# The last block's k and v computed in absent steps of the recurrent block's first and last turns

## What is computed

```python
x = _L0_xattn_ref(x, ctx_2048, ...)    # grouped attention, layer norm
x = _L1_xattn_ref(x, ctx_2048, ...)    # non-local block with batch statistics
x = _L2_xattn_ref(x, ctx_2048, ...)    # recurrent block: projections, scan, feed-forward
x = _L3_xattn_ref(x, ctx_2048, ...)    # cross attention and MLP

def _L3_xattn_ref(hidden_states, encoder_hidden_states, ...):
    q = (layer_norm(hidden_states, ln1_w, ln1_b) @ q_w + q_b)     # 16 heads of 32
    k = (encoder_hidden_states @ k_w + k_b)                       # the context, not x
    v = (encoder_hidden_states @ v_w + v_b)
    attn = softmax(where(mask, q k^T / sqrt(32), finfo.min))
    hidden = (attn @ v) @ cproj_w + cproj_b + hidden_states
    y = gelu(layer_norm(hidden, ln2_w, ln2_b) @ fc_w + fc_b) @ proj_w + proj_b
    return hidden + y
```

## Time and profile before

| what | us |
|---|---|
| median of 3 runs | 4407.73 |
| range of the 3 runs | 4401.81 to 4412.48 |
| the profiled execution | 4404.54 |
| its span | 4402.8 |
| PE busy in it | 4084.0 (93%) |
| DVE busy | 2325.2 (53%) |
| ACT busy | 1502.5 (34%) |
| POOL busy | 1423.2 (32%) |

### The profile page before, as it was taken

The page is one execution under the profiler, slowest core; times in us unless marked ns, Lnnn a source line. Parts: engine busy times, 40 slices in busy tenths (PEclk is TensorE's granted clock), DMA queues, the critical chain, the costliest instruction groups (busy, mean ns, idle before and its releaser), DMA issues. The chain is left out here.

```text
span 4402.8 us, 79945 instructions
## 1 busy us (share of the span) xinstructions
PE 4084.0 (93%) x30944; PEld 2520.5 (57%) x30944; DVE 2325.2 (53%) x2689; ACT 1502.5 (34%) x2622; POOL 1423.2 (32%) x1181
## 2 busy tenths in 40 slices
PE   6999999994799999999999997789999999999998
PEld 5666666663566666666666664345444444544443
DVE  4666666662577767776666774343333333333320
ACT  2555555552333443344333332112222221222210
POOL 2433333431554555455444542121111111111110
PEclk8999999997899999999999998899999999999999
DMA  3121212113001000010000000300000000000000
GB/s 100 59 68 66 68 58 68 61 44 124 21 19 38 26 26 26 26 36 26 26 26 26 26 25 11 147 21 1 30 20 10 30 1 30 1 30 8 22 10 10
DMA packets 102765, 161.50 MB, mean 37 GB/s; under 512 B 17264, under 2 KB 34800, under 8 KB 101936
## 3 DMA queue, kind: packets, MB, share of 16 engines
q1 hardware_dynamic: 102448, 156.59, 10.5%
HBM read 106.20 MB, written 41.94 MB: 34 GB/s over the span
## 5 line engine op out<-in xcount | busy, mean ns | idle before, releaser
L1410 DVE COPY_PREDICATED b_A<-b_mask,b_pS 128x2048 f32<-128x2048 uint32 x128 | 458.3, 3580 | 184.2 <-PE b_pS L1124 183.2
L1862 PE MATMUL c_pR<-c_proj_w,c_fcT 128*128 128x512 f32 x1024 | 459.5, 597 | 7.5 <-ACTq L1701 3.8
L1796 PE MATMUL c_pR<-c_xT,c_fc_w 128*128 128x512 f32 x1024 | 458.2, 595 | 7.5 <-PEq L1701 2.4
L695 POOL TENSOR_TENSOR a_S<-a_S,a_negmax 128x2048 f32<-128x2048 f32 x64 | 231.1, 3610 | 500.0 <-DVE a_negmax L629 500.0
L2013 POOL TENSOR_TENSOR c_S<-c_S,c_negmax 128x1024 f32<-128x1024 f32 x64 | 121.4, 1897 | 701.3 <-DVE c_negmax L1960 701.3
L1563 POOL TENSOR_TENSOR b_R<-b_R,b_Wh 128x512 f32<-128x512 f32 x192 | 228.4, 1190 | 356.9 <-PE b_pS L1124 356.5
L1986 DVE TENSOR_TENSOR c_res<-c_res,c_pR 128x512 f32<-128x512 f32 x128 | 88.0, 687 | 482.8 <-PE c_pR L1862 449.4
L1124 PE MATMUL b_pS<-b_R,b_kT 32*128 32x128 f32 x7168 | 271.2, 288 | 77.1 <-ACT b_A L1264 36.3
L1796 PEld LDWEIGHTS c_pR<-c_xT,c_fc_w 128*128 128x128 f32 x1024 | 191.4, 190 | 244.5 <-issue 240.7
L1873 ACT ACTIVATE c_fcT<-c_pR,c_vec 128x512 f32<-128x512 f32 x128 | 88.0, 687 | 698.3 <-PE c_pR L1796 658.1
L1862 PEld LDWEIGHTS c_pR<-c_proj_w,c_fcT 128*128 128x128 f32 x1024 | 189.7, 190 | 238.4 <-issue 228.0
(11 more groups left out here) (228 smaller groups left out, 7921.5 us busy)
## 6 DMA issues: line engine op xcount, KB each, us to landing
a_c<-ctx SPq DMA_DIRECT2D x16, 512.0 KB, 4.0
a_x<-x SPq DMA_DIRECT2D x16, 512.0 KB, 5.0
a_kexp<-a_kT SPq DMA_DIRECT2D x512, 16.0 KB, 1.8
a_xl<-x SPq DMA_DIRECT2D x32, 256.0 KB, 2.6
a_cl<-ctx SPq DMA_DIRECT2D x32, 256.0 KB, 2.8
mid_x<-a_xl SPq DMA_DIRECT2D x32, 256.0 KB, 2.9
mid_wy<-a_wy SPq DMA_DIRECT2D x32, 256.0 KB, 2.1
b_x1g<-mid_x SPq DMA_DIRECT2D x16, 512.0 KB, 4.1
```

What stands on the lines that cost most here:

```text
L695: nc.gpsimd.tensor_tensor(S[n % 2][:, :, :], S[n % 2][:, :, :], negmax[n % 2][:, :].unsqueeze(2).to_broadcast([P, RH, T]), ALU.add)\
L1410: nc.vector.copy_predicated(A[:, :, :].rearrange("p q (n two h) -> p q n two h", two=2, h=h)[:, :, :, 1, :], masks[h][:, :].bitcast(U32).r ...
L1796: mm = nc.tensor.matmul(bank, w[:, c, at * P:at * P + P], src[:, c, :], start=(c == 0), stop=(c == KC - 1))
L1862: mm = nc.tensor.matmul(bank, fcT[part % 2][:, m, g * T:g * T + T], proj_w[:, KC * part + m, :], start=(m == 0), stop=(m == KC - 1))
```

## The change

`phase_a` stores every transposed context tile `cT` in DRAM. `phase_b` computes all 32 K and 32 V fills of the last layer in places of absent steps: 24 in turns -1, 0 and 1 (groups 0 to 2), 40 in turns 15 and 16 (groups 3 to 7). Such a unit takes an absent step's bank of the ring; PE fills it from the stored `cT` rows, the step's own engine drains it with the bias, and SP stores it. V units take places that DVE drains, K units places that ACT drains. For the early units k_w and v_w lie in the buffers of `Wfk` and `Wfr`, the context rows in those of `Wfv` and `Wo`, and the weights `Wo`, `Wfk`, `Wfr`, `Wfv` are loaded after the last early unit (turn 1). For the late units k_w and v_w are loaded over `Wk` and `Wr` after turn 14's scan. `phase_c` loads finished k and v instead of the context, and loses the steps `cT`, `k` and `v`.

The units by place: in turn -1, seven before the step n1 (two V, then five K), V after shift, V before a0, two K before k0, one V each inside k0 and after td, two K before b1, three K at fk0, fk1 and fr0; in turn 0 four V (fv0, fv1, o0, o1); in turn 1 two V (fv0, fv1). In turn 15, 21 units in slots 3 to 15 (none in slots 0 to 2, 4, 8, 16 and 17). In turn 16, eleven before the step gate, one K each at k0 and td, two K at w and two V at b0 before n2, two V at b1 after n2.

```diff
+            def store_cT(j):
+                wait(out(j, "cT", 1))
+                sp.dma_start(dram["cT"][bass.ds(j.times(1), 1), :, :, :].rearrange("b p k n -> p (b k) n"), cT[:, :, :]).then_inc(*cT_stored.up(16))
...
                 if has(i + 1):
                     load_mask(i + 1, 1 - par)
                     spread_k(i + 1, 1 - par)
+                    store_cT(i + 1)
...
+                        if s == "cT":
+                            act.wait_ge(*cT_stored(j + -1, 16))
...
+    EARLY, LATE = (-1, 0, 1), (N - 1, N)
+    OUT_SLOTS = 6
+    def absent(turn):
+        return [(name, who) for kind, step in table if not 0 <= turn + LAG[kind] < N for name, who in fills(kind, step)]
+    def share(turns, first, groups):
+        left = {g: {"K": list(range(KC)), "V": list(range(GC))} for g in range(first, first + groups)}
+        order = []
+        for turn in turns:
+            for name, who in absent(turn):
+                window = sorted(left)[:2]
+                for kind in "VK" if who == "dve" else "K":
...
+            def load_kv(side):
+                sp.dma_start(kv_k[side][:, :, :], dram["L3_xattn_k_w"].rearrange("(k p) n -> p k n", p=P)).then_inc(*kv_weights["K"].up(16))
+                first = sides[side][0][3][1]
+                load_group(side, first)
+                sp.dma_start(kv_v[side][:, :, :], dram["L3_xattn_v_w"].rearrange("(k p) n -> p k n", p=P)).then_inc(*kv_weights["V"].up(16))
+                sp.dma_start(kv_rows[side], dram["rows_c"][:, 0:D]).then_inc(*kv_weights["V"].up(16))
+                load_group(side, first + 1)
...
             load(Turn(None))
+            load_kv(0)
             load_state(Turn(None), 0)
...
+            turn(Turn(None, add=N - 2), 0, True)
+            before = Turn(None, add=N - 1)
+            wait(x2_saved.all(before))
...
+            wait(S_.full(before + -1, "s", G - 1, SLOTS - 1))
+            load_kv(1)
...
+            def unit(at, name, side, n):
+                _, _, _, (kind, group, m) = sides[side][n]
+                for free in Ring.ready(R_, at, name):
+                    pe.wait_ge(*free)
+                bank = pR[:, R_.at[name] % RING, :]
+                pe.wait_ge(kv_weights[kind].sem, (16 if kind == "K" else 32) * (side + 1))
+                pe.wait_ge(*groups_loaded(side, group))
+                if kind == "K":
+                    for h in range(2):
+                        for c in range(KC):
+                            mm = nc.tensor.matmul(bank[:, h * TOK:h * TOK + TOK], kv_k[side][:, c, m * P:m * P + P], half_of(side, group, h)[:, c, :],
+                                                  start=(c == 0), stop=(c == KC - 1))
+                else:
+                    h, at_ = divmod(m * T, TOK)
+                    for c in range(KC):
+                        mm = nc.tensor.matmul(bank, half_of(side, group, h)[:, c, at_:at_ + T], kv_v[side][:, c, :], start=(c == 0), stop=(c == KC - 1))
+                mm.then_inc(*R_.filled.up())
...
-    TABLE = """F0 hb F1 cT w1 F2 k0 F3 k1 n1 R0 k2 q0 R1 k3 s0 q1 R2 v0 s1 R3 v1 F4 t0 s2 v2 F5 v3 t1 p0 s3 F6 F7 t2 p1
+    TABLE = """F0 hb w1 F1 F2 F3 n1 R0 q0 R1 q1 s0 R2 s1 R3 F4 t0 s2 F5 t1 p0 s3 F6 F7 t2 p1
...
+            def load_k(j):
+                if (j + -1).exists():
+                    wait(scored(j + -1, NU))
+                sp.dma_start(kT[:, :, :], dram["k"][bass.ds(j.times(1), 1), :, :, :].rearrange("b p k n -> p (b k) n")).then_inc(*k_loaded.up(16))
...
                 if has(i + 2):
-                    wait(full(i + 1, "n2", KC - 1))
-                    load_context(i + 2)
+                    load_k(i + 2)
+                    load_v(i + 2)
                     wait(limit_sign(i + 1, 1))
                     load_mask(i + 2)
```

More of the change, by code:

```diff
@@ L876, in take_groups, with unit_out, stores_done, run @@
             return [pR[:, R_.bank(name, g), :] for g in range(G)]
-        def run(eng, scan, project, finish, who=""):
+        def unit_out(eng, at, name, side, n):
+            eng.wait_ge(*R_.filled(at, R_.at[name] + 1))
+            nth, slot = divmod(n, OUT_SLOTS)
+            if nth:
+                eng.wait_ge(*stores(slot, side, nth))
+            return pR[:, R_.at[name] % RING, :], kv_slots[side][n % OUT_SLOTS]
+        def stores_done(eng):
+            for slot in range(OUT_SLOTS):
+                eng.wait_ge(*stores(slot, 1, 0))
+        def run(eng, scan, project, finish, who="", unit=None):
             def skip(at, kind, step):
@@ L900, in turn @@
                         else:
+                            if unit is not None and static and i.add == 1 and (kind, step) == ("f", "gn_mean"):
+                                stores_done(eng)
                             (project if kind in "pl" else finish)(i + LAG[kind], (par + LAG[kind]) % 2, step)
@@ L986, in turn, with mixed, has @@
                         load_state(i + 2, par)
-            for i in (-1, 0, 1):
-                turn(Turn(None, add=i), i % 2, True)
+            def mixed(n):
+                i = Turn(None, add=n)
+                def has(j):
+                    return 0 <= j.add < N
+                for kind, step in table:
+                    if not has(i + LAG[kind]):
+                        for name, _ in fills(kind, step):
+                            if (n, name) in unit_at:
+                                store_unit(n, name)
+                            if (n, name) == sides[0][-1][0:2]:
+                                wait(R_.filled(i + 1, R_.at[name] + 1))
+                                for w in ("Wo", "Wfk", "Wfr", "Wfv"):
+                                    load_weights(loaded_f, W[w], "L2_%sT" % w)
+                    if (kind, step) == ("p", "stats"):
+                        if has(i + -2):
+                            store(i + -2)
+                        if has(i + -1):
+                            back(i + -1)
+                        if has(i + 1):
+                            save(i + 1)
+                    if (kind, step) == ("p", "w") and has(i + 2):
+                        load(i + 2)
+                        if has(i):
+                            load_state(i + 2, n % 2)
+            for n in EARLY:
+                mixed(n)
             with sp.Fori(0, (N - 4) // 2) as reg:
@@ L992, in _ @@
                     turn(Turn(reg, 2, 2 + u), u, False)
-            for i in range(N - 2, N + 2):
-                turn(Turn(None, add=i), i % 2, True)
+            turn(Turn(None, add=N - 2), 0, True)
+            before = Turn(None, add=N - 1)
+            wait(x2_saved.all(before))
+            wait(xn_ready[0].all(before))
+            wait(R_.full(before, "w", 1))
+            wait(R_.full(before, "r", 1))
+            wait(r_joined.all(before + -1))
+            wait(S_.full(before + -1, "s", G - 1, SLOTS - 1))
+            load_kv(1)
+            for n in LATE:
+                mixed(n)
+            turn(Turn(None, add=N + 1), 1, True)
+            for slot in kv_stored:
+                sp.wait_ge(slot.sem, slot.seen)
             sp.wait_ge(*stored.all(Turn(None, add=N - 1)))
@@ L1304, in finish, with unit @@
                     nc.scalar.activation(rt[:, g, :], bank, ACT.Tanh, scale=0.5).then_inc(*R_.emptied["act"].up())
-            run(act, scan, project, finish, "act")
+            def unit(at, name, side, n):
+                _, _, _, (kind, group, m) = sides[side][n]
+                if side and n < OUT_SLOTS:
+                    act.wait_ge(*xm_ready.all(Turn(None, add=N - 1)))
+                bank, dst = unit_out(act, at, name, side, n)
+                nc.scalar.activation(dst, bank, ACT.Identity, bias=col("L3_xattn_k_b", m)).then_inc(*R_.emptied["act"].up())
+            run(act, scan, project, finish, "act", unit)
         @block.vector
@@ L1813, in step @@
                     linear(j, s, W["q_w"], n, xT1, "n1")
[L1814 to L1818 removed]
                 elif s[0] == "s":
                     c, pair_ = divmod(n, 2)
+                    if n == 0:
+                        pe.wait_ge(*k_loaded(j, 16))
                     pe.wait_ge(*(masked(j, n) if n else masked.before(j)))
```

169 lines of the change are left out of this document (114 added, 55 removed).

## The result

The changed kernel takes 4332.16 us (median of 4 runs, 4323.25 to 4340.87) against 4404.77 for the kernel before beside it: a ratio of 0.9834, 95% interval 0.9816 to 0.9852. The forecast was 4328. The profiled execution took 4340.87 us (span 4339.1) and is the longest of the four, so its parts add up to more than the median.

What follows compares the result with a forecast made beforehand. PE's stream bounds phase_c's turn 0 and phase_b's middle turns; a DVE, ACT and POOL chain bounds phase_b's edges. 4404.54 - 220.6 (phase_c) + 141.3 (phase_b) = 4325.2 us profiled, median 3.2 above: 4328 (4302 to 4366).

Steps and rivals of the forecast that it cites:

- Turn -1: phase_b's turn -1 grows by 44.2 us (38 to 55), with n1 coming 26.2 us later.
- turns 0 and 1: phase_b's turns 0 and 1, with six units, grow by 1 us each (0 to +8 and -1 to +7).
- A unit: PE's time for one moved K or V unit: 3.5 us, so 224 us for 64 (219 to 238).
- Turns 15 and 16: phase_b's end: turn 15 grows by 47.5 us (43 to 57), turn 16 by 47.6 (44 to 56).
- The cT stores: phase_a's 16 stores of cT cost nothing; if SP were late, under 0.5 us a turn, 8 in all.
- phase_c's middle turns: Seven turns of phase_c lose 204.3 us of fills, less 2 us for newly exposed waits: 202.3 us gained.
- phase_c's first stage: phase_c's turn -1, up to the fourth score step: a gain of 18.3 us (14 to 22).
- rival A: PE's clock falls to 0.66 in phase_c's first stage: +28 us, 4356; chance 0.07.
- B: phase_c's middle turns are no longer PE's; n1 or transposes wait 5 us a turn: +35, 4363; chance 0.08.
- C: phase_b's edges hide nothing and the moved units cost all 224 us: 4411, no change; chance 0.03.
- D: In phase_c, loads of k and v delay the x rows by 20 us beyond slack each turn: 4468; chance 0.03.
- E: phase_b's edges hide more: all 99.4 us idle and some 12 of clock go, growth 112, 4299; chance 0.04.

Runs made afterwards that it cites:

- quarter units: The changed kernel with each of the 64 units doing only the first of its four input blocks, all loads, drains and stores kept: 4199.78 us.

## Why the prediction was right, by its own steps

**What bounds the kernel.** Right: the moved work hid where PE had idled, and only there. Turn -1 grew 2.1 us more than the sum, turns 0 and 1 3.8 less. Part of how near the total came is luck, though: the changed kernel's own executions lie 18 us apart, and between executions the end of the same phase_a moves by up to 9 us.

**A unit.** A V unit of 8 records takes 3.6 us in the clean stretches (two in 7.03), as did a K unit: 3.5 was right.

**Turn -1.** The first unit came at 67.35 of 67 (behind phase_a's end moved by 3.5), n1 at +26.4 of +26.2. Behind n1 it was +19.9 of +18.0: I had POOL's 3.2 us stay (2.38 measured). Of idle time 11.8 us went and not 12.7, and by difference the clock gave back 6.8 and not 7.8.

**Turns 15 and 16.** +45.6 and +49.8 of +47.5 and +47.6: their sum is off by 0.3. The quarter units show how it comes about: the first quarter of the late work, 35 us, cost 4.3, since it fell into idle time, and the rest 91.7 of 105, since little was left to fill. I had expected 87 for that rest, from the same working.

**The cT stores** at nothing: right within 7 us, which is what that run can tell.

**phase_c's middle turns.** The fills went with their price and n1 stayed clear as worked out (2.8 us for "some 3"). The term that was mis-sized is "2 us for newly exposed waits": it was 10.2 (204.3 less 194.1). The six waits before F0 are 6.9 of it, the slow clock of turn 0's first four F fills 1.9 (15.94 us for 14.0, and 14.0 when the same kernel ran again). The waits come from k and v in flight as the loop closes. No row of before shows them: there the q8 packets came as well, nine a turn, and those of the loop's end had landed 0.5 us or more before F0.

**phase_c's first stage.** 12.1 for 18.3, the largest miss for its size (that of the middle turns is 8.2 of 202.3). I let POOL start 3.6 us earlier for 1.4 MB less ahead of cproj_w; it started 1.4 earlier, counted from the last fv (35.2 for 36.6), which is 2.2 of the 6.2 us missed. From there to q0 it was 7.7 us for 6.8, and from q0 to the fourth score step 21.6 for 18.4. The clock accounts for these two: rival A happened in small. The clock in 10 us before n1 and the 10 behind it, in the changed kernel and then in the kernel before:

```profile
2951.50:2961.50 10.00, 0.00 (x0) 0.00 (x0) 2.20 (x5) 0.00 (x0) 2.40 (x4) 0.50 1.04 417
2961.50:2971.50 10.00, 9.00 (x24) 5.51 (x24) 4.95 (x2) 3.11 (x4) 4.63 (x1) 0.55 1.02 397
```

```profile
2807.10:2817.10 10.00, 7.72 (x20) 2.98 (x17) 7.17 (x19) 1.38 (x2) 2.49 (x4) 1.00 1.04 411
2817.10:2827.10 10.00, 9.59 (x34) 5.00 (x35) 4.96 (x2) 4.00 (x6) 4.64 (x1) 1.00 1.02 404
```

Without cT and k there PE idles 31 us before n1, and what follows runs at a granted clock of 0.50 to 0.55, the lower level (1.2 GHz) for most of it. The removed fills had also borne the start themselves (cT took 3.24 us at 2804.20, while POOL still waited). The price here is the 3.68 less 1.97 and the 5.81 less 3.6, about 4 us, and not the 28 of rival A, since the clock was back by the second q fill (3.67 us). It fell once more behind the next wait:

```profile
2981.15 1.97 PE L2032 MATMUL c_pR<-c_ident,c_S 128*128 128x128 f32 x8 [2.50 <-POOL c_S L2199]
```

The same shape takes 1.06 at full speed (2842.86 in the kernel before). Where the clock was back sooner, with the early units cut to a quarter, q0 took 3.67 and q0 to the fourth score step 18.1 us, for a forecast of 18.4. The 4.5 us given to the chain of DVE and POOL came out right there, and what it lacked is the clock.

**The rivals.** B (n1 late) and C (nothing hidden) didn't happen, D (x rows late) and E (more hidden) neither; A happened with a seventh of its price. The misses of phase_c (11.0), phase_b (1.1) and phase_a (3.5) are the 15.7 us (rounding aside) by which the profiled execution (4340.87) exceeds the sum of 4325.2; some of that is the execution itself, since the median lies 8.7 below it.

## What to carry to other kernels

Work moved into idle stretches is worth what the same stretch shows as PE's idle time, piece by piece; a sum over the pieces came within some 2 us in each turn here, but for turns 0 and 1 together (3.8), and executions of one kernel differ by as much. Look also at what the removed work had covered: here it kept PE busy at a phase's start, and without it the clock was at half for the first steps that counted. And before new loads are put at a loop's end, see in the DMA rows whether a queue of instruction loads moves packets there.

## What the runs showed of the hardware

A loop of PE with some 1,600 matmul and weight records a turn (801 of each above) is brought anew in every turn (nine packets of 16 KB) or hardly at all, as it lies: 144 increments of a semaphore ahead of it left 5 packets in six turns, and 24 records fewer none in five. The reload costs nothing by itself and 0.5 to 2.5 us a turn with 2 MB of data in flight. And PE's clock moves between executions of the same code: a stretch at the end of turn 14 took 39.9 us at 0.91 in the changed kernel's profile and 37.1 at 1.00 when it ran again, with 333 PE instructions in both. phase_a's last PE work, with the same code, started between 1035.2 and 1044.5 us; nothing here says why.
